# Softmax division of a windowed attention: from PE transposes and VectorE to a path over DRAM, with the low parts of x on GpSimd

## The reference, cut to what matters

```
scores = q k^T * scale + bias, masked          # per head, blocks of 128 queries by 256 keys
p      = softmax(scores)
o      = p v                                   # [16 heads, 512, 16]
x1     = layernorm(x + o w_out)
```

## Time and profile before

| | us |
|---|---|
| median of 3 runs | 1004.26 (1003.01 to 1005.67) |
| the profiled execution, own time | 1004.63 |
| its span, first to last instruction | 1002.9 |
| busy PE / DVE / ACT / POOL | 915.2 / 719.0 / 575.9 / 407.6 |
| mean granted TensorE clock | 0.953 of full |

### The profile page before, as it was taken

The page is one execution under the profiler, slowest core; times in us unless marked ns, Lnnn a source line. Parts: engine busy times, 40 slices in busy tenths (PEclk is TensorE's granted clock), DMA queues, the critical chain, the costliest instruction groups (busy, mean ns, idle before and its releaser), DMA issues.

```text
span 1002.9 us, 25924 instructions
## 1 busy us (share of the span) xinstructions
PE 915.2 (91%) x9500; PEld 753.2 (75%) x9500; DVE 719.0 (72%) x2795; ACT 575.9 (57%) x1167; POOL 407.6 (41%) x687
## 2 busy tenths in 40 slices
PE   3587879999999999999999999999999989889994
PEld 2375668878788878788878787878787867668884
DVE  7766576877777777777777778787878673327885
ACT  5144556555656565656565656565756464325886
POOL 5142443354444444444444444444444353101443
PEclk9577889999999999999999999999999999899998
DMA  7634443535454545444544454444444400121764
GB/s 257 168 117 121 129 140 126 151 120 143 135 140 137 138 138 139 139 137 139 134 143 133 144 129 146 129 147 129 146 108 145 124 28 22 42 91 49 221 202 132
DMA packets 93534, 131.86 MB, mean 131 GB/s; under 512 B 12128, under 2 KB 47584, under 8 KB 93408
## 3 DMA queue, kind: packets, MB, share of 16 engines
q1 hardware_dynamic: 93136, 129.95, 44.2%
q10 hardware_dynamic: 272, 0.26, 0.1%
HBM read 79.31 MB, written 50.33 MB: 129 GB/s over the span
## 4 chain that ended last, share of the span: by engine, by line
PE 64%; DVE 25%; ACT 5%; issue 4%; POOL 2%; DMA 0%; ACTq 0%; DVEq 0%; POOLq 0%
PE bank L921 29%; DVE bank L689 11%; PE bank L909 11%; PE bank L940 8%; PE bank L975 7%; PE bank L961 3%; DVE max_q L689 3%; DVE qk_parts L661 2%; PE bank L983 2%; DVE gate L738 2%; DVE gate L736 1%; PE bank L1016 1%; PE bank L1029 1%; ACT Pt L643 1%; DVE stats L877 1%
## 5 line engine op out<-in xcount | busy, mean ns | idle before, releaser
L689 DVE CUSTOM_DVE_ANT_0 bank<-bank,mask 128x256 f32<-128x256 f32 (+1 forms) x1024 | 369.3, 423 | 136.1 <-PE bank L940 134.5
L448 ACT ACTIVATE Pt<-bank 128x512 f32<-128x512 f32 (+1 forms) x512 | 248.2, 536 | 204.1 <-PE bank L961 204.0
L347 POOL TENSOR_SCALAR_AFFINE_SELECT Pt<-Pt 128x512 f32<-128x512 f32 x256 | 174.7, 682 | 414.8 <-ACT Pt L448 414.8
L940 PE MATMUL bank<-Ks,Qs 59*128 59x256 f32 (+1 forms) x1024 | 149.5, 320 | 51.3 <-DVE max_q L689 40.5
L940 PEld LDWEIGHTS bank<-Ks,Qs 59*128 59x128 f32 x1024 | 108.5, 192 | 94.8 <-DVE max_q L689 54.5
L689 DVE DVE_READ_ACCUMULATOR2_ANT max_q<- 128x1 f32 x1024 | 144.6, 141 | 0.0
L349 POOL TENSOR_SCALAR_AFFINE_SELECT Pt<-Pt 128x384 f32<-128x384 f32 x256 | 139.3, 544 | 0.0
L975 PE MATMUL bank<-Pt,Vp 128*32 128x256 f32 (+1 forms) x2048 | 131.2, 377 | 0.0
L921 PE MATMUL bank<-x1T,Wg 64*128 64x512 f32 x960 | 128.0, 398 | 0.8 <-DVE o_tok L703 0.8
L921 PE MATMUL bank<-cT,Ug 64*128 64x512 f32 x960 | 125.8, 393 | 0.0
L961 PE MATMUL bank<-Qs,Ks 60*128 60x256 f32 (+1 forms) x1024 | 112.1, 271 | 0.4 <-ACT Pt L448 0.3
(11 more groups left out here) (111 smaller groups left out, 1345.7 us busy)
## 6 DMA issues: line engine op xcount, KB each, us to landing
parts_dram<-qk_parts SPq DMA_DIRECT2D x128, 256.0 KB
Qs<-parts_dram SPq DMA_DIRECT2D x128, 128.0 KB, 2.6
Ks<-parts_dram SPq DMA_DIRECT2D x128, 128.0 KB, 2.7
xt_raw<-in_xt SPq DMA_DIRECT2D x16, 512.0 KB, 4.2
Qs<-parts_dram SPq DMA_DIRECT2D x128, 64.0 KB, 2.6
Ks<-parts_dram SPq DMA_DIRECT2D x128, 64.0 KB, 2.7
x_res<-in_x SPq DMA_DIRECT2D x16, 512.0 KB, 3.9
x_dram<-y SPq DMA_DIRECT2D x16, 512.0 KB, 3.7
```

The source lines that it names most:

```text
L347: gp.affine_select(out=p4[:, :, 0:128], in_=p4[:, :, 0:128], compare_op=ALU.is_ge, fill=0.0, base=0, pattern=[[0, 4], [1, 128]], channel_m ...
L448: sc.activation(probabilities(g, 2 * pair + odd)[:, S * a:S * a + n], SC[odd][:, 0:n], ACT.Exp).then_inc(exp_done, 1)
L689: ins = ve.tensor_tensor_reduce(out=raw, in0=raw, in1=mask[:, keys], scale=1.0, scalar=MASKED, op0=ALU.add, op1=ALU.max, accum_out=max_q[: ...
L940: ins = te.matmul(MX[odd][:, 256 * (n % 2):256 * (n % 2) + 256][:, keys], Qs[rows, 2 * g + pair, n * WIN:(n + 1) * WIN], Ks[rows, 2 * g + ...
```

## The change

For the first 15 sequences (the last keeps the old path, in functions named `last_...`):

- PE no longer turns contexts: `ctx_transpose` and `o_transpose` go, and so does `normalise` on DVE.
- SP stores each `ctx_raw` to DRAM (`store_ctx`), and ACT's next `ctx_out` waits for that store, where it waited for the transposes. SP then loads the sums (`load_denominators`, four small DMAs) and the contexts without them (`load_contexts`, two) in the head-major layout that the projection wants. DVE turns the sums into a dense layout, inverts them and turns them back. SP stores the inverses, and loads each of them into 16 partitions (`spread_inverses`). POOL multiplies (`scale_contexts`), and ACT and DVE split the product into `oT` as before, now from SBUF.
- The high and low part of x for sequence t+2 is made in iteration t (ACT in slots 11 and 12, POOL after its windows), where t+1's was made, by ACT and DVE, in slots 1 and 2.
- DVE's `update` of the recurrence is cut in two, `forget` (its first instruction, moved to an earlier slot) and `take_in`.
- `Wo` and `Uo` are no longer split before the loop, but in `last_sequences`, into the place of `Win`.

The diff, cut to its core:

```diff
@@ sync @@
+            def store_ctx(t, g):
+                wait(sp, ctx_done, 4, t, g + 1)
+                sp.dma_start(ctx_dram[t % 2, g], ctx_raw[:, :]).then_inc(ctx_stored[g], 16)
+            def load_denominators(t):
+                sp.wait_ge(den_cleared, 1)
+                for g in range(QUADS):
+                    wait(sp, ctx_stored[g], 16, t, 16)
+                wait(sp, inv_stored, 16, t - 1, 16)
+                rows = ctx_dram[t % 2].rearrange("g (h r) (q i) -> q (g h) r i", r=2 * D, i=128)[:, :, D, :]
+                for q in range(4):
+                    sp.dma_start(den_q[32 * q:32 * q + H, :], rows[q]).then_inc(den_in, 16)
+            def load_contexts(t, c):
+                wait(sp, otlo_done, 2, t - 1, c + 1)
+                rows = ctx_dram[t % 2, 2 * c:2 * c + 2].rearrange("g (h r) s -> (g h) r s", r=2 * D)[:, 0:D, :]
+                sp.dma_start(o_un[:, c, :], rows).then_inc(o_un_in[c], 16)
+            def store_inverses(t):
+                wait(sp, inv_turned, 1, t, 1)
+                sp.dma_start(inv_dram[t % 2].rearrange("r (q i) -> q r i", i=128), den_q[:, :]).then_inc(inv_stored, 16)
+            def spread_inverses(t):
+                wait(sp, inv_stored, 16, t, 16)
+                for c in range(KC):
+                    wait(sp, scaled_done, 2, t - 1, c + 1)
+                    rows = inv_dram[t % 2, 8 * c:8 * c + 8]
+                    sp.dma_start(inv_den[:, c, :], rows.unsqueeze(1).to_broadcast([8, D, S])).then_inc(inv_in[c], 16)
             def iteration(t):
                 if p1: max_to_stack(t - 1, 3)
                 if now: stack(t, 1)
...
+                if by_rows: store_ctx(t - 1, 1)
                 if real(t + 2): load_xt(t + 2)
                 if now:
                     stack(t, 2)
                     max_to_stack(t, 0)
-                    stack(t, 3)
+                if by_rows: store_ctx(t - 1, 2)
+                if now: stack(t, 3)
                 if n1: parts_to_dram(t + 1, 0)
                 if now: max_to_stack(t, 1)
+                if by_rows: store_ctx(t - 1, 3)
...
+                if by_rows:
+                    load_denominators(t - 1)
+                    for c in range(KC):
+                        load_contexts(t - 1, c)
                 if n1: stack(t + 1, 0)
                 if now: max_to_stack(t, 2)
-                if n1: parts_to_dram(t + 1, 1)
+                if by_rows:
+                    store_inverses(t - 1)
+                    spread_inverses(t - 1)
+                if n1:
+                    parts_to_dram(t + 1, 1)
+                    store_ctx(t, 0)
@@ gpsimd @@
+            def scale_contexts(t, c):
+                wait(pool, o_un_in[c], 16, t, 16)
+                wait(pool, inv_in[c], 16, t, 16)
+                gp.tensor_tensor(o_un[:, c, :], o_un[:, c, :], inv_den[:, c, :], ALU.mult).then_inc(scaled_done, 1)
             def iteration(t):
+                if p2 and t - 2 < B - 1:
+                    for c in range(KC):
+                        scale_contexts(t - 2, c)
...
                     for hh in range(2, 4):
                         window(t, 0, hh)
+                    if real(t + 2):
+                        for c in range(KC):
+                            x_lo(t + 2, c)
@@ scalar @@
             def ctx_out(t, g, bank):
                 wait(act, pv_ready, 4, t, g + 1)
-                wait(act, ct_ready, 4, t, g)
+                pt, pg = before(t, g)
+                if pt < B - 1:
+                    wait(act, ctx_stored[pg], 16, pt, 16)
...
                 sc.activation(ctx_raw[:, :], bank[:, :], ACT.Copy).then_inc(ctx_done, 1)
+            def last_weights_hi():
+                act.wait_ge(last_weights_in, 32)
+                act.wait_ge(v_ready, 2 * B)
+                sc.activation(out_stage[:, 1, :], out_stage[:, 1, :], ACT.Copy, scale=0.5).then_inc(u_o_halved, 1)
+                sc.activation(Wo[:, 0, :, :], out_stage[:, 0, :]...).then_inc(last_hi, 1)
+                act.wait_ge(u_o_halved, 1)
+                sc.activation(Uo[:, 0, :, :], out_stage[:, 1, :]...).then_inc(last_hi, 1)
@@ vector @@
                 if n1: qk_lo(t + 1, 2, B0)
                 attend(13)
+                if p1: turn_denominators(t - 1)
                 if n1: qk_lo(t + 1, 3, B1)
-                if p1: normalise(t - 1, 3, A0)
-                if p2:
-                    x1_lo(t - 2, 0, B0)
-                    x1_lo(t - 2, 1, B1)
+                if p1: invert_denominators(t - 1)
+                if p2: x1_lo(t - 2, 0, B0)
+                if p1: turn_inverses(t - 1)
+                if p2: x1_lo(t - 2, 1, B1)
@@ tensor @@
                     values(t - 1, 1, A1)
-                    wait(pe, maxrow_done, 4, t - 1, 4)
-                    ctx_transpose(t - 1, 0, A0)
-                if p2:
-                    wait(pe, gate_done, 6, t - 3, 1)
-                    o_transpose(t - 2, 0, B0)
-                    freed(pe, (gate_done, 6, t - 3, 2), (ctx_done, 4, t - 1, 1))
-                    o_transpose(t - 2, 1, B1)
 
                 attend(1)
                 if p3:
                     g2, g3 = gate_halves(2, A0), gate_halves(3, A1)
-                    wait(pe, o_done, 4, t - 1, 1)
+                    wait(pe, maxrow_done, 4, t - 1, 4)
                     wait(pe, ctx_done, 4, t - 1, 2)
                     abreast(g2, g3, 0, None)
```

More of the change, by code:

```diff
@@ L161, in build @@
         STAGED = ((Wout, w_stage[:, 1536:2048]), (Wg, w_stage[:, 2048:3584]),
-                  (Wo, w_stage[:, 3584:4096]), (Ug, gate[:, 0:3, :].rearrange("p a b -> p (a b)")), (Uo, ctx_raw[:, :]))
+                  (Ug, gate[:, 0:3, :].rearrange("p a b -> p (a b)")))
         def real(t):
@@ L270, in iteration @@
                 p1, p2, n1, now = real(t - 1), real(t - 2), real(t + 1), real(t)
+                by_rows = p1 and t - 1 < B - 1
                 if p1: max_to_stack(t - 1, 3)
@@ L389, in _ @@
                 iteration(t)
+                if t == B:
+                    for n, w in enumerate((Wo, Uo)):
+                        pool.wait_ge(last_hi, n + 1)
+                        gp.tensor_tensor(w[:, 1, :, :], out_stage[:, n, :].rearrange("p (c n) -> p c n", c=KC),
+                                         w[:, 0, :, :].bitcast(F32), ALU.subtract).then_inc(last_lo, 1)
             def second(t, rnd, i):
@@ L606, in _ @@
                 qk_hi(0, k, banks[4 + (k + 2) % 4])
-            act.wait_ge(weights_in, 80)
-            for n in range(5):
+            act.wait_ge(weights_in, 48)
+            for n in range(3):
                 weights_hi(n)
@@ L776, in iteration @@
                     qk_lo(t + 1, 1, B1)
+                if p3: forget(t - 3, 1)
                 attend(7)
-                if p3: update(t - 3, 0)
+                if p3: take_in(t - 3, 0)
                 attend(8)
-                if p3: update(t - 3, 1)
-                if p1: normalise(t - 1, 2, B0)
+                if p3: take_in(t - 3, 1)
                 attend(9)
@@ L798, in last_sequences @@
                 (A0, A1), (B0, B1) = pairs_of(B)
-                normalise(t, 0, A0)
-                ot_lo(t - 1, 0, B0)
-                ot_lo(t - 1, 1, B1)
+                last_normalise(0, A0)
+                ot_lo(t - 1, 0)
+                ot_lo(t - 1, 1)
                 residual(t - 1, 0, B0)
@@ L978, in values, with last_ctx_transpose @@
                 ins.then_inc(pv_ready, 1)
-            def ctx_transpose(t, g, bank):
-                wait(pe, ctx_done, 4, t, g + 1)
+            def last_ctx_transpose(g, bank):
+                wait(pe, ctx_done, 4, B - 1, g + 1)
                 for n in range(NB):
@@ L1201, in last_sequences @@
                 scores(t, 2, 3)
+                wait(pe, gate_done, 6, t - 2, 1)
                 project_out(t - 1, 0, B0)
+                wait(pe, gate_done, 6, t - 2, 2)
                 project_out(t - 1, 1, B1)
@@ L1213, in last_sequences @@
                 scores(t, 3, 2)
-                wait(pe, o_done, 4, t, 2)
-                ctx_transpose(t, 2, MX[0])
+                pe.wait_ge(o_done, 2)
+                last_ctx_transpose(2, MX[0])
                 scores(t, 3, 3)
@@ L1225, in last_sequences @@
                 gate_of_input(t - 1, 1, A1)
-                wait(pe, o_done, 4, t, 3)
-                ctx_transpose(t, 3, MX[0])
+                pe.wait_ge(o_done, 3)
+                last_ctx_transpose(3, MX[0])
                 gate_of_state(t - 1, 0, A0)
```

198 lines of the change are left out of this document (120 added, 78 removed).

## The result

The changed kernel takes 1116.1 us (median of four runs, 1109.0 to 1121.9) against 1004.4 for the kernel before: a ratio of 1.111, interval 1.104 to 1.118. It is 112 us slower; the forecast was 54 slower, and the time lies above the range. Medians are of all runs of a kernel; the ratios leave out one run each of experiments 1, 3 and 5, over 1.5% longer than that kernel's fastest, and the profile of experiment 3 is of such a run.

A forecast was written before the change was run, and what follows sets the result against it. PE's work was taken to bound the kernel; per iteration -3.0 (transposes) -0.9 (maxima) +6.0 (stall) +1.9 (clock) = +4.0 us, 14 times +56, and -2 outside, took 1004.63 to 1058 us; 8-in-10 range 1008 to 1092.

The forecast's parts named there:

- The stall at slot 1: PE's gate product waits for ACT's context copy, held by group 0's store behind the parts: 6.0 us per iteration, bounds 4.5 to 9.
- The clock: After each pause PE runs 3.9 us at half rate, losing 1.9 us per iteration, bounds 0 to 3.4.
- The transposes: PE's context and o transposes go from each iteration, with nothing hiding them: 3.0 us gained, 14 times.
- the three small operations of VectorE: DVE's two turns and one inversion, 0.3 us each, fitting in the time that `normalise` gives back.
- PE's wait for maxima: PE's 1.0 us wait per iteration for DVE's maxima shrinks by 0.9, bounds 0 and 1.0, as DVE is relieved.
- Landing of 64 KB: Inverses' store, issued at S + 2.45 (S: start of PE's x1 transposes), lands after 2.6 us, bounds 2.0 and 3.7.
- when PE needs it: PE's gate product taking bank A1 could start at S + 10.9, S being the start of PE's x1 transposes.
- SP gets 13 issues ... on a queue that has pauses like that: SP's added issues, about 0.44 us each, 5.7 us per iteration, counted as hidden in the queue's pauses.
- They cost nothing: POOL's two multiplications precede group 2's windows, whose values product comes five slots later: no cost; up to 2.6 without cover.
- inverses come late too: Rival: inverses 3 us later would stop DVE, then PE: 14 times +3 more, 1100 us; chance 0.06.
- Outside the loop: Iteration 1 -2.0, `last_sequences` -1.0 and +1.8, two loads gone at the start -0.8: together -2.0 us.
- The four rivals with a smaller cost: No clock loss 1032 (0.14), store beside the parts 976 (0.12), stall and clock evening out 1003 (0.04), all stores hidden 948 (0.02).

The follow-up runs named there:

- run 1: Changed kernel with the store of group 0's context issued ahead of the inverses' store, its spreads and the four parts: 1030.5 us.
- experiment 3: Changed kernel with the four parts and the store of group 0's context issued ahead of the inverses' store and spreads: 1046.5 us.
- run 5: Changed kernel with 28 extra matmuls on PE in slot 1, in the pause before the gate products: 1095.1 us.
- run 2: Changed kernel with two buffers for the raw context, SP's order untouched: 1026.8 us.
- Run 11: Changed kernel with only the two loads of raw contexts moved on SP, to the end behind parts and context store: 1104.0 us.
- run 8: Changed kernel with context store early, parts and context loads ahead of the inverses' spreading, next group 0's stack ahead of the denominators: 1088.9 us.

## Why the prediction was right in kind and half the size

- **The stall at slot 1: right.** Place, releaser, SP's order and the single buffer are as forecast, and runs 1 and 2 take it away from two sides. Its size is 7.6 in the iteration shown and 7.0 on average (91.0 / 13), where 6.0 was the value and 4.5 to 9 the bounds. It comes thirteen times, not the fourteen of the sum: iteration 2 has no gate product in slot 1. There ACT waits 6.6 us for the store all the same (133.38), and PE 3.7 us for the exponentials behind that copy (134.52), as the prediction says of a PE with another bank.
- **The clock: right.** 1.9 forecast; 1.8 by the rows, 1.6 by run 5.
- **The transposes: right.** 3.0 us, and the three small operations of VectorE are 0.31, 0.53 and 0.30 us where 0.3 each was taken. Of PE's wait for maxima half comes back, not 0.9.
- **The step "Landing of 64 KB": mis-sized.** 2.6 us (bounds 2.0 to 3.7) against 4.0 at the median and 4.9 in the rows shown. The nearest rows were of DMAs with no such loads ahead of them. The change puts 0.5 MB of contexts there, and the stack behind them. Run 11 takes the contexts away and measures 2.45, so the 2.6 was right for a queue without them. With the parts at S + 9.1 in place of S + 6.0, the rest of the count holds: 11.3 us from the parts to the landing, 10.2 forecast.
- **The step "when PE needs it", S + 10.9: wrong, and it hid that error.** PE was there at S + 13.6 (543.39 less the wait of 7.62), since it waits on its way: 1.0 us inside the transposes of x1 and 1.5 at scores for the rows of maxima. Both stood in the sum at nothing. The stall is a difference of two late times and came out nearly right by luck; but the two waits are lost time themselves. They are the largest part of what the forecast lacks, 2.4 of 4.8 us of this iteration; the larger stall is 1.6.
- **"SP gets 13 issues ... on a queue that has pauses like that": failed.** I priced SP's issues by their own 5.7 us against its idle time, and what they put on the queue at nothing. The loads of contexts lie ahead of the rows of maxima: SP issues these at 523.15, PE gets them at 529.55, and run 11 takes away most of that wait. SP also waits: some 2 us for the landing of the fourth context, and 3.4 at the median (4.3 in the rows above) for the inverses, ahead of the parts and the next stack. In run 1 the waits for rows and keys together are 3.2 us of each iteration (33.8 us in 10.7).
- **"They cost nothing" of GpSimd's two multiplications: true in the changed kernel, with less to spare than I said.** The reason I gave (values product five slots later) missed ACT's copy between them. Runs 3 and 8 show 2.3 and 6 us of waiting when the inverses come later. The rival "inverses come late too" named VectorE; the way that exists goes over ACT.
- **Outside the loop: -2.0 forecast, not borne out.** Ahead of the first block of x1 transposes 5.2 us are lost, which holds iteration 2 with its 3.7 us; behind the last block 0.9 are gained. The single terms were not measured.

The four rivals with a smaller cost had 0.32 between them and none was near. Late inverses, at 1100 the nearest in time, are not what happened in this kernel. The Trainium skill (DMA: Bandwidth & Descriptors, "Two DMAs through the same engine are not ordered") says that within one queue of one DMA engine descriptors start in order, though they may end otherwise. Runs 8 and 11 agree: GpSimd starts on the first spreading load 3.8 or 9.3 us after its issue, and the inverses' store lands in 2.45 or 4.0, by what was issued before them.

## What to carry to other kernels

Price a DMA on a shared queue by what is issued ahead of it in the changed order, not by a row in which it travels alone, and count the waits of the issuing engine as well as its issues. For a chain that leaves the core and comes back, write down each deadline on the queue, and order the queue by them; here the order on SP and of three operations on VectorE took 1116 us to 994, with the same operations. A stall that is a difference of two times can come out right while both are wrong: check the early one too.

## What was not expected of the hardware

- A DMA behind large ones takes their time: GpSimd started 3.1 us after the issue of the second spreading load in the changed kernel, on what the first had brought, and 8.7 after it behind the parts and the contexts (run 8).
- Filling a pause of 7.6 us with 28 useless matmuls made the kernel 21 us faster, and left the pause's cause in place.
- In run 11 the low clock grew by 29 us while the pause stayed as long as it was; what decides between a stretch of 6.8 and one of 10.2 us at 1.2 GHz stays open.
